# Moving one more product of a selective scan to GpSimd, splitting its Silu in two, and moving low-part subtractions around the first FFN

## The reference, cut to what matters

```python
def step(h, inp):
    d_l, b_l, c_l, x_l = inp
    h = jnp.exp(d_l[:, :, None] * A) * h + (d_l * x_l)[:, :, None] * b_l[:, None, :]
    y_l = jnp.einsum('ben,bn->be', h, c_l)
    return (h, y_l)
...
y = ys.transpose(1, 0, 2) + x * W_D
y = y * jax.nn.silu(skip)
return resid + y @ out_w.T
```

## Time and profile before

| | us |
|---|---|
| median of three runs | 1954.39 (1948.84 to 1954.95) |
| the profiled execution's own time | 1948.66 |
| its span, first to last instruction | 1946.7 |
| scan (Mamba), from DVE's first scan to the end of its last | 42.5 to about 930 |
| first FFN starts | 942.3 |

### The profile page before, as it was taken

The page is one execution under the profiler, slowest core; times in us unless marked ns, Lnnn a source line. Parts: engine busy times, 40 slices in busy tenths (PEclk is TensorE's granted clock), DMA queues, the critical chain, the costliest instruction groups (busy, mean ns, idle before and its releaser), DMA issues. The chain is left out here.

```text
span 1946.7 us, 26915 instructions
## 1 busy us (share of the span) xinstructions
...
## 2 busy tenths in 40 slices
...
DMA packets 57363, 97.97 MB, mean 50 GB/s; under 512 B 10928, under 2 KB 11056, under 8 KB 57136
## 3 DMA queue, kind: packets, MB, share of 16 engines
...
## 5 line engine op out<-in xcount | busy, mean ns | idle before, releaser
L380 POOL TENSOR_TENSOR m_U<-m_U,m_C 128x1024 f32<-128x1024 f32 x256 | 603.6, 2367 | 58.6 <-DVE m_U L878 48.2
L517 PEld LDWEIGHTS m_y<-ident,m_U 128*128 128x128 f32 x2048 | 248.5, 146 | 116.7 <-issue 74.1
L878 DVE TENSOR_TENSOR_SCAN m_U<-m_dA,m_carry,m_U 128x512 f32<-128x512 f32 x256 | 311.9, 1264 | 7.1 <-ACT m_dA L749 6.6
L878 DVE TENSOR_TENSOR_SCAN m_U<-m_dA,m_U 128x512 f32<-128x512 f32 x256 | 296.5, 1203 | 14.5 <-ACT m_dA L749 11.0
L517 PE MATMUL m_y<-ident,m_U 128*128 128x128 f32 x2048 | 280.2, 282 | 26.8 <-POOL m_U L380 26.8
L749 ACT ACTIVATE m_dA<-high,m_negA 128x512 f32<-128x512 f32 x256 | 172.8, 685 | 84.1 <-DVE m_U L878 83.7
L749 ACT ACTIVATE m_dA<-even,m_negA 128x512 f32<-128x512 f32 x256 | 171.2, 684 | 64.5 <-DVE m_U L878 62.9
L1084 POOL TENSOR_TENSOR SW<-g_Rt 128x1024 f32<-128x1024 f32 x16 | 31.6, 1997 | 258.3 <-ACT g_Rt L1270 258.3
L501 PE MATMUL m_psB<-m_stack,m_pick 128*128 128x512 f32 x208 | 105.8, 508 | 59.6 <-DVE m_U L861 59.2
L1265 ACT ACTIVATE g_sil<-g_psG 128x512 f32<-128x512 f32 x96 | 57.5, 599 | 156.2 <-PE g_psG L1144 156.0
L1265 ACT ACTIVATE f_sil<-f_psG 128x512 f32<-128x512 f32 x96 | 57.5, 599 | 149.6 <-PE f_psG L1144 149.2
...
## 6 DMA issues: line engine op xcount, KB each, us to landing
m_C<-bc_rows SPq DMA_DIRECT2D x256, 256.0 KB, 3.2
...
```

What stands on the lines that cost most here:

```text
L380: pool.tensor_tensor(u, u, C[:, M % C_RING, :].unsqueeze(1).to_broadcast([P, PE_E, CHUNK]), ALU.mult).then_inc(hc_ready, 1)
L517: last = nc.tensor.matmul(y[:, t, j * P:(j + 1) * P], U[:, M % U_RING, j, t * P:(t + 1) * P], ident[:, :], start=False, stop=n == N - 1, i ...
L878: nc.vector.tensor_tensor_scan(u, dA[:, s % A_RING, :], u, carry[:, e, n:n + 1] if q else 0.0, ALU.mult, ALU.add).then_inc(scan_done, 1)
```

## The change

- `ON_POOL` has a tuple for each half: states 3, 7, 10, 14 in the first and 4, 9, 14 in the second. POOL's B products of a chunk are units 3, 7, 10, 14, 20, 25, 30: seven.
- `silu` becomes two parts. `silu_x` stays in unit 13. `silu_g` (the gate) goes to unit 2; for chunk 0 it is in unit 10. Each part has its own pair of table loads.
- The last unit's C product goes to DVE, which waits for its own scans; PE and POOL wait for it (`last_product`).
- At the end of the scan PE's `last_out(0, 0)` is moved ahead of `nsum(253)`, and `last_out(1, 0)` behind `nsum(255)`; part `back1` of the last chunk goes from unit 30 to 29.
- Low part 1 is subtracted at the end of the scan, behind part 0. In the FFN, part 2 comes first, and part 3 after DVE has finished the coefficients (`C_ready`). PE waits for the low parts before block 8 and before the output products.

```diff
-    ON_POOL, AHEAD = (4, 9, 14), 3
+    ON_POOL, AHEAD = ((3, 7, 10, 14), (4, 9, 14)), 3
...
-    pool_units = [M for M in range(ALL_UNITS) if M % N in ON_POOL]
+    pool_units = [M for M in range(ALL_UNITS) if M % N in ON_POOL[M % UNITS // N]]
...
-                    if name == "silu":
-                        if k + 1 < CHUNKS:
-                            silu_x(k + 1)
-                        silu_gate(k)
+                    if name[:4] == "silu" and (name, k) != ("silu_g", 0):
+                        (silu_x if name == "silu_x" else silu_gate)(k)
                         nc.scalar.preload_act_table_set(EXP_LN_SET)
...
+            M = ALL_UNITS - 1
+            dve.wait_ge(C_ready[M % C_RING], 16 * (M // C_RING + 1))
+            dve.wait_ge(scan_done, PE_E * ALL_UNITS)
+            u = U[:, M % U_RING, :, :]
+            nc.vector.tensor_tensor(u, u, C[:, M % C_RING, :].unsqueeze(1).to_broadcast([P, PE_E, CHUNK]),
+                                    ALU.mult).then_inc(last_product, 1)
             part("gate1", CHUNKS - 1)
...
-            pool.wait_ge(hi_ready, 1)
-            pool.tensor_tensor(shared.weights[1][:, 0, :], shared.even[:, 0, :],
-                               shared.weights[0][:, 0, :].bitcast(FP32), ALU.subtract)
+            pool.wait_ge(last_product, 1)
+            for i in range(2):
+                pool.wait_ge(hi_ready, i + 1)
+                pool.tensor_tensor(shared.weights[1][:, i, :], shared.even[:, i, :],
+                                   shared.weights[0][:, i, :].bitcast(FP32), ALU.subtract)
...
-                low(1)
-                chunk(0, meanwhile=low)
+                low(2)
+                chunk(0)
+                pool.wait_ge(C_ready, 1)
                 low(3)
...
-                    if start and i in (KH // 2, KH):
-                        pe.wait_ge(w_low, 2 * i // KH)
+                    if start and i == KH:
+                        pe.wait_ge(w_low, 1)
```

More of the change, by code:

```diff
@@ L173, in mamba @@
                  "late": [(at + d, name, k) for k, at in ((8, 8), (9, 11), (10, 21), (11, 24))
-                          for d, name in ((0, "turn0"), (0, "turn1"), (2, "query"))]}
-        ACT_AT = {0: ("turn0", "turn1"), 1: ("in0",), 3: ("cv0",), 4: ("in1", "back2"), 5: ("back3",), 6: ("cv1",),
[1 row of a table removed]
+                          for d, name in ((0, "turn0"), (0, "turn1"), (2, "query"))] + [(29, "back1", CHUNKS - 1)]}
+        ACT_AT = {0: ("turn0", "turn1"), 1: ("in0",), 2: ("silu_g",), 3: ("cv0",), 4: ("in1", "back2"), 5: ("back3",),
[1 row of a table added]
                   15: ("out0",), 16: ("low",), 18: ("bc",), 19: ("bl", "dt0"), 20: ("sk0", "dl0"), 21: ("dt1",),
@@ L190, in mamba @@
         BEHIND = {"out0": -1, "out0+": -1, "out1": -1, "out1+": -1, "gate1": -1, "back2": -1, "back3": -1,
-                  "gate0": 0, "back0": 0, "back1": 0, "silu": 0, "sum": 2, "square": 2, "factors": 2, "norm": 2, "double": 2}
+                  "gate0": 0, "back0": 0, "back1": 0, "silu_g": 0, "sum": 2, "square": 2, "factors": 2, "norm": 2, "double": 2}
         ASKED = dict(enumerate((4, 1, 5, 0), CHUNKS))
@@ L198, in parts_of @@
             late = [(name, k) for slot, name, k in at["late"] if c == CHUNKS - 1 and slot == i]
-            return [(name, k) for name, k in chunks if 0 <= k < CHUNKS] + late
+            chunks = [(name, k) for name, k in chunks if 0 <= k < CHUNKS and (name, k) != ("back1", CHUNKS - 1)]
+            return chunks + late
         def tile_of(k, j):
@@ L276, in _ @@
                     sp.wait_ge(rows_out, 16 * (c + 1))
-                if n in ON_POOL:
+                if n in ON_POOL[p]:
                     i = BEFORE[M]
@@ L378, in _ @@
                     pool.wait_ge(carry_ready, UNITS * (c // 2) + N * p + n + 1)
-                pool.wait_ge(C_ready[M % C_RING], 16 * (M // C_RING + 1))
-                pool.tensor_tensor(u, u, C[:, M % C_RING, :].unsqueeze(1).to_broadcast([P, PE_E, CHUNK]),
-                                   ALU.mult).then_inc(hc_ready, 1)
+                if M < ALL_UNITS - 1:
+                    pool.wait_ge(C_ready[M % C_RING], 16 * (M // C_RING + 1))
+                    pool.tensor_tensor(u, u, C[:, M % C_RING, :].unsqueeze(1).to_broadcast([P, PE_E, CHUNK]),
+                                       ALU.mult).then_inc(hc_ready, 1)
                 if (M + AHEAD) in pool_units:
@@ L513, in nsum @@
                                              start=t % 2 == 0 and j == 0, stop=False, skip_group_check=True)
-                pe.wait_ge(hc_ready, M + 1)
+                if M < ALL_UNITS - 1:
+                    pe.wait_ge(hc_ready, M + 1)
+                else:
+                    pe.wait_ge(last_product, 1)
                 for t in range(TILES):
@@ L568, in _ @@
                         pe.wait_ge(free[b], HEAD_TAKEN[b])
+                if M == ALL_UNITS - 1:
+                    last_out(0, 0)
                 if M >= 2:
                     nsum(M - 2)
-            last_out(0, 0)
             nsum(ALL_UNITS - 2)
+            nsum(ALL_UNITS - 1)
             last_out(1, 0)
-            nsum(ALL_UNITS - 1)
             pe.wait_ge(scan_done, PE_E * ALL_UNITS)
```

16 lines of the change are left out of this document (10 added, 6 removed), and 3 rows, old and new, of the table ACT_AT.

## The result

| | before | after |
|---|---|---|
| median of four runs each, us (lowest to highest) | 1952.32 (1948.84 to 1954.95) | 1930.66 (1925.06 to 1936.52) |
| ratio, 95% interval | | 0.989 (0.9854 to 0.9927) |
| the profiled execution, and its span, us | 1948.66, 1946.7 | 1932.65, 1930.9 |

What follows compares the result with a forecast made beforehand. DVE was taken to set the pace, POOL second. Gains of 20.4 (chunks), 0.2 (scan's end) and 5.0 (first FFN) made 25.6 us: 1923.1 from the profiled execution, 1928.8 from the median, middle 1926, range 1915 to 1941.

Steps and rivals of the forecast that it cites:

- One product less, and the wait at unit 5: DVE behind gate1: a B product of 1.11 us leaves each chunk, and the wait of 0.88 or 1.00 goes.
- Silu split: ACT's waits at unit 15 shrink by 1.92 us per chunk; about 0.3 of unit 2's new 4.47 us block shows.
- Rival 3: ACT's table loads: a drain at every load costs 2.7 us more in 7 chunks; gain 7, 1944 us; chance 0.04.
- The wait behind gate0 stays, since the second half's states are the same.: DVE's wait for PE behind gate0, mid-chunk, was to stay as before, with no gain or loss counted.
- POOL in even chunks: POOL runs nearly without pause from unit 7; waits for it cost 1.2 us per even chunk, 1.8 at unit 30.
- Rival 1: POOL becomes the bound in even chunks, which lose 14.7 us against the sum; gain 11, 1941 us; chance 0.14.
- Chunk 0: The gate's Silu in unit 10 was to cost 0.9 us, ACT's idle 1.9 taking most of the added 2.57.
- End of the scan: DVE's gate1 comes about 1.4 us earlier, but POOL's two subtractions leave a gain of 0.2, bounds 0 and 1.4.
- First FFN: Most of PE's 4.07 us wait for coefficients goes and its clock recovers; gain 5.0, bounds 2 and 6.5.
- Rival 2: The block in unit 2 isn't hidden, costing up to 4.47 us in each of 7 chunks; 1957 us; chance 0.05.
- Rival 4: Waits at unit 5 and in the FFN stay because PE carries them; gain 15, 1937 us; chance 0.15.

Runs made afterwards that it cites:

- e1_pool: The kernel before with ON_POOL alone changed, so seven B products on POOL; 1937.6 us, ratio 0.9921.
- e2_silu: The kernel before with the Silu alone split, the gate's part in unit 10 for chunk 0; 1950.6 us, ratio 0.9988.
- e8_silu_unit5: The changed kernel with the gate's Silu of chunks 1 to 7 at the end of unit 5 instead of unit 2; 1951.7 us, ratio 1.0005.
- e6_unit19: The changed kernel with unit 19's B product on POOL instead of unit 20's; 1916.4 us, ratio 0.9815.
- e9_eight: The changed kernel with four B products on POOL in both halves of a chunk, eight in all; 1923.8 us, ratio 0.9852.
- e4_first_gate: The changed kernel with chunk 0's gate Silu in unit 13, sharing table loads with chunk 1's Silu of x; 1927.7 us, ratio 0.9869.
- e7_both: The changed kernel with the edits of e4_first_gate and e6_unit19 joined; 1913.1 us, ratio 0.9776.
- e10_row_first: e4_first_gate with PE issuing unit 21's spread row ahead of the skip products and unit 16's sum; 1915.3 us, ratio 0.9813.
- e11_row_five: e10_row_first with unit 21's spread row written five times over; 1916.5 us, ratio 0.9799.
- e3_tail: The changed kernel with the B products and the gate's Silu as in the kernel before; 1950.3 us, ratio 0.9986.
- e5_low_back: The changed kernel with the low parts at their old points, the last product still on DVE; 1932.0 us, ratio 0.9894.

## Why the prediction was right, and where its terms were off

The forecast was 1926 with a range of 1915 to 1941, faster at 0.9; it is faster, at 1930.7. The mechanism held in the main, but that the sum came this near is in part luck: one step failed, and other terms were too cautious by nearly as much. Its terms one by one, in the profiled execution, which took 9.6 us more than the 1923.1 forecast for it. Chunks 1 to 6 gained 16.8 for 19.0, chunk 7 1.8 for 2.3, chunk 0 -4.0 for -0.9, the stretch ahead of them 0.8 for nothing, the scan's end 0.3 for 0.2, the first FFN 3.5 for 5.0, and the rest lost the 3.4 that are not the change's.

**One product less, and the wait at unit 5.** Forecast 1.11 + 0.88 or 1.00 per chunk. `e1_pool` shows it alone: 2.1 by unit 16 in chunks 1 to 6. Right.

**Silu split.** Forecast 1.92 per chunk less 0.3 over all; measured 1.8 in each of chunks 1 to 6, by units 12 to 16 of `e2_silu`. ACT's wait at unit 15 is 0.29 and 0.47 for 0.18 and 0.35. Right. The sum was not in step with its own text, which put what shows of the block in unit 2 at 0.3 in each chunk and took 0.1 in the odd ones, nothing in chunks 2 and 6, and 0.8 in chunk 4; measured are the 0.19 and 0.53 above, and nothing in chunk 4. Rival 3, a drain at every load, is out: in `e8_silu_unit5` load, Silu, load and the next decay follow from 402.03 to 406.56 with no gap, 4.5 us. The Trainium skill (ScalarE: Activation LUTs, What ACT_TABLE_LOAD costs) has about 1.38 us of drain more for each load, an estimated 7.2 us for the block; these rows don't agree with it.

**"The wait behind gate0 stays, since the second half's states are the same."** This step failed. The states were the same, but not PE's clock: 1.6 us more in chunks 2, 3 and 5, 4.9 together. That PE's clock can be low behind an idle time stands in my own working for the FFN (0.56 behind 4.07 us); I didn't ask it of gate0.

**POOL in even chunks.** Forecast 1.2 each and a wait of 1.8 at unit 30. Measured: 0.86 there in chunk 4, as before, and the chunk ends 3.9 ahead. POOL's idle time ahead of the carry copies, the 7.3 of the earlier trace rows, is what paid, as the groups of POOL's lines in chunk 4 after show:

```profile
L383 POOL TENSOR_TENSOR m_U<-m_U,m_C 128x1024 f32<-128x1024 f32 x32 | 75.8, 2368 | 2.5
L346 POOL TENSOR_TENSOR m_U<-even,m_B 128x1024 f32<-128x1024 f32 x7 | 16.6, 2365 | 0.0
L379 POOL COPY m_carry<-m_U 128x2 f32<-128x2 f32 x31 | 5.9, 191 | 1.4 <-DVE m_U L890 1.4
```

Of it 1.4 is left. POOL's waits at unit 30 are 0.85 to 0.89 in chunks 2, 4 and 6, against 0.84 to 0.88 before, so the term was over-sized by all of its 1.2 per chunk, 3.6 in all. With the 0.8 of chunk 4 that hid most of the 4.9 above; that is the luck in the sum. The 0.65 and 0.32 us that chunks 2 and 6 lose at the border go with waits of 0.54 for PE's spread row, not for POOL. How near the edge was shows in `e6_unit19`: with 1.0 more closed on DVE, POOL's wait grows by 1.05 to 1.91. Rival 1 is out for this kernel, and `e9_eight` shows it one step further.

**Chunk 0.** Forecast -0.9, bounds -1.5 and +1.5; measured -4.0, of which 0.7 stood before unit 4. I counted ACT's idle time as if the block could use it, but the block stands ahead of a drain that PE waits for. With the block gone, in `e4_first_gate`, the 3.9 us behind it are gone by unit 16.

**End of the scan**: 0.2 forecast, 0.3 measured, set by POOL. **First FFN**: 5.0 forecast, 3.5 measured. PE's wait for the coefficients fell from 4.07 to 0.54, and the output products begin earlier. PE's timeline at both points:

```profile
953.32 0.63 PE L1197 MATMUL f_psU<-ident,SW 128*128 128x128 f32 x4 [0.54 <-DVE SW L1405]
...
959.68 0.39 PE L1234 MATMUL f_psO<-weights_hi,f_H_hi 128*128 128x256 f32 x1 [0.25 <-POOL weights_lo L1116]
```

The output products stand 33.1 us behind the FFN's start instead of 37.4. The 1.5 that are missing lie at its first matmuls, those of hidden block 0, which take 4.5 us for 2.9; PE had waited 2.49 us at the FFN's border (1.31 before), and its clock was 0.72 from 926 to 932. PE's timeline there after:

```profile
926.83 1.08 PE L1161 MATMUL f_psG<-zs,weights_hi 128*128 128x512 f32 x2 [2.49 <-DVE f_pause L1468]
```

and in `e6_unit19`:

```profile
912.73 0.73 PE L1161 MATMUL f_psG<-zs,weights_hi 128*128 128x512 f32 x2 [2.49 <-DVE f_pause L1468]
```

`e6_unit19`, `e7_both`, `e10_row_first` and `e11_row_five` have the same code there and the same wait, but PE's clock at 2.4 GHz; their second addition comes 50.3 us behind the FFN's start, 5.1 sooner than before. So the term was right in size for an execution whose clock is up at that point.

**Rival 2** (the block in unit 2 isn't hidden) is out but for the 0.53 in chunk 7. **Rival 4** (waits at unit 5 and in the FFN stay) is out: at unit 5 at most 0.24 us is left in chunks 1 to 6, in the FFN 0.54.

What stays open is when PE's clock falls. Over all fourteen profiled executions, 18 of 182 groups of skip products behind a gate in chunks 0 to 6 were slow. All 18 stood behind idle times of 1.82 to 2.16 us, but 36 others stood behind 1.8 us or more and took 2.05, and the FFN's start ran at 2.4 GHz behind 2.49 us in four kernels of nine. Idle time ahead is thus a sign and no rule.

At gate0 of chunks 1 to 6 none of 18 was slow in the three kernels with the long wait at unit 15 and this order of PE's queue (before, `e1_pool`, `e3_tail`), and 15 of 30 in the five with the Silu split (after, `e2_silu`, `e4_first_gate`, `e5_low_back`, `e8_silu_unit5`). It is likely that the long wait at unit 15 used to draw the slow stretch to a place where nothing waited for PE: before has its clock down at unit 16 or 17 of chunks 1, 2, 5 and 6. These rows and this window of chunk 2 show it behind an idle time of 2.62 us. It wasn't tested by itself.

```profile
323.50 0.50 PE L501 MATMUL m_psB<-m_stack,m_pick 128*128 128x512 f32 x1 [2.62 <-DVE m_U L861]
323.84 2.98 PE L410 MATMUL m_job<-high,late 128*128 128x512 f32 x4
...
325.45:327.45 2.00, 2.00 (x6) 0.50 0.52 114
```
